# One product for each block of scores in a perceiver's third attention over its context

## The reference

```python
q = x_n @ Wq.T                      # 512 x 256, 16 heads of 16
k, v = split(ctx @ Wkv.T)           # 1601 keys of each batch, 16 heads of 16
p = softmax(q_h @ k_h.T * 16**-0.5) # for each batch and head: 64 x 1601
x = x + concat(p @ v_h) @ Wo.T
```

## Time and profile before

| | |
|---|---|
| median of 3 runs | 2267.64 us (2262.94 to 2269.9) |
| profiled execution, its own time | 2266.19 us |
| its span, first to last instruction | 2264.4 us |
| mean granted TensorE clock | 0.955 |
| PE busy | 2049.1 us (90%) |
| DVE busy | 1389.0 us (61%) |
| ACT busy | 1131.4 us (50%) |
| POOL busy | 507.4 us (22%) |
| score passes, lines 611 to 613 on `cTh`, `cTl`, all three attentions | 768 each, 276.2 + 268.4 + 268.8 us |
| value passes, same lines on `pTh`, `pTl` | 1248 each, 383.5 + 348.4 + 348.0 us |

### The profile page before, as it was taken

The page is one execution under the profiler, slowest core; times in us unless marked ns, Lnnn a source line. Parts: engine busy times, 40 slices in busy tenths (PEclk is TensorE's granted clock), DMA queues, the critical chain, the costliest instruction groups (busy, mean ns, idle before and its releaser), DMA issues. The chain is left out here.

```text
span 2264.4 us, 42645 instructions
## 1 busy us (share of the span) xinstructions
PE 2049.1 (90%) x15334; PEld 1775.2 (78%) x15334; DVE 1389.0 (61%) x2707; ACT 1131.4 (50%) x2279; POOL 507.4 (22%) x410
## 2 busy tenths in 40 slices
PE   5887999999887998489899999987979999999898
PEld 2765999999666875287799999966859999997687
DVE  7465777777455453721677777745447777775466
ACT  3245666666423432321566666624446666664254
POOL 2322222221012420101322222012332122220034
PEclk9798999999997998789999999999989999999999
DMA  5153101100141213531101100002220010000022
GB/s 214 37 237 118 45 31 32 44 30 0 36 149 58 99 34 138 214 146 56 45 31 36 40 30 30 0 17 72 75 93 32 31 43 32 30 15 0 19 79 77
DMA packets 32317, 144.06 MB, mean 64 GB/s; under 512 B 3632, under 2 KB 9136, under 8 KB 28848
## 3 DMA queue, kind: packets, MB, share of 16 engines
q1 hardware_dynamic: 32176, 142.23, 17.5%
HBM read 125.59 MB, written 13.90 MB: 62 GB/s over the span
## 5 line engine op out<-in xcount | busy, mean ns | idle before, releaser
L1021 ACT ACTIVATE pTh<-ps 128x512 fp32r<-128x512 f32 (+1 forms) x768 | 353.9, 519 | 384.2 <-PE ps L921 382.0
L1079 DVE TENSOR_TENSOR pTl<-ps,pTh 128x512 fp32r<-128x512 f32 (+1 forms) x768 | 416.0, 583 | 128.4 <-ACT pTh L1021 128.1
L611 PE MATMUL ps<-pTh,ch 128*128 128x256 f32 (+1 forms) x1248 | 383.5, 307 | 2.6 <-DVE pTl L1079 2.5
L612 PE MATMUL ps<-pTl,ch 128*128 128x256 f32 (+1 forms) x1248 | 348.4, 279 | 0.0
L613 PE MATMUL ps<-pTh,cl 128*128 128x256 f32 (+1 forms) x1248 | 348.0, 279 | 0.0
L611 PE MATMUL ps<-cTh,qh 128*128 128x512 f32 (+2 forms) x768 | 276.2, 360 | 20.7 <-POOL ql L875 13.5
L613 PE MATMUL ps<-cTh,ql 128*128 128x512 f32 (+2 forms) x768 | 268.8, 350 | 0.0
L612 PE MATMUL ps<-cTl,qh 128*128 128x512 f32 (+2 forms) x768 | 268.4, 349 | 0.0
L1066 DVE TENSOR_REDUCE top<-ps 128x1 f32<-128x802 f32 x192 | 189.4, 986 | 111.1 <-PE ps L613 111.1
L611 PEld LDWEIGHTS ps<-pTh,ch 128*128 128x128 f32 (+1 forms) x1248 | 235.1, 188 | 16.7 <-DVE pTl L1079 12.8
L612 PEld LDWEIGHTS ps<-pTl,ch 128*128 128x128 f32 (+1 forms) x1248 | 235.7, 189 | 0.0
(11 more groups left out here) (349 smaller groups left out, 3645.1 us busy)
## 6 DMA issues: line engine op xcount, KB each, us to landing
w<-l1f_w_in SPq DMA_DIRECT2D x16, 1024.0 KB, 8.2
raw<-ctxT_in SPq DMA_DIRECT2D x16, 801.0 KB, 4.2
raw<-ctx_in SPq DMA_DIRECT2D x14, 832.0 KB, 4.5
wg<-l0f_guide_in SPq DMA_DIRECT2D x10, 704.0 KB, 5.1
z<-ctx_in SPq DMA_DIRECT2D x8, 832.0 KB, 12.8
z<-z SPq DMA_DIRECT2D x8, 832.0 KB, 10.8
keys<-ctx_in SPq DMA_DIRECT2D x8, 832.0 KB, 10.2
zT<-zT SPq DMA_DIRECT2D x8, 801.0 KB, 8.8
```

The lines of the kernel that those rows point to most:

```text
L611: pe.matmul(out, high, moving_high, start=start, stop=False)
L612: pe.matmul(out, high, moving_low, start=False, stop=False)
L1021: nc.scalar.activation(pTh[0:w, PARTS[g][0]:PARTS[g][0] + n, slot, :], ps[0:w, turned_bank[slot][g], 0:n * P].rearrange("p (k r) -> p k r" ...
L1079: dve.tensor_tensor(pTl[0:w, at, slot, :], ps[0:w, turned_bank[slot][g], 0:n * P].rearrange("p (k r) -> p k r", r=P), pTh[0:w, at, slot, : ...
```

## The change

Only `l3x` changes. The first and second of the three attentions go on using `cross_attention`.

- **Real keys.** Keys of a batch are projected: `project_keys` multiplies the transposed context by `wk`, three passes for each of 8 tiles (2 chunks of 128 key features, 4 tiles of some 400 keys). ACT copies a tile out of PSUM bank 7 (`keep_key`), POOL splits it (`split_key`), and SP moves it.
- **The stack.** Two heads have 32 key features together. `stacked` holds for each pair of heads 96 rows: the high part, the high part again, the low part. `move_half` fills them with 12 DMAs of 32 rows from SBUF to SBUF, 48 a batch. `stacked` exists once, so a chunk's moves wait until its four units are scored.
- **The queries.** Each pair's query is repeated three times in the rows of the product (`wq` is laid out so), and ACT or DVE copies it out of PSUM twice, masked for either head (the last operation of each: `tensor_scalar` or `activation` with a mask as scale). `stage` makes rows 0 to 31 high, 32 to 63 low and 64 to 95 high. One matmul over 96 rows then gives high·high + low·high + high·low.
- **Order.** In a couple PE runs `key_tile` 0 ahead of `values(1)`, behind a wait for `low(1)` since both use bank 7, and `key_tile` 1 behind the odd scores. ACT's two `keep_key` stand behind second keep 3. The last batch has no tiles.
- **Raw context.** POOL does both parts of its split; ACT's copies go. The transposed context has one buffer instead of two.
- **Setup.** The two dense steps become one block in which PE makes 8 query products and 8 key tiles of batch 0; the first scores wait for all 48 moves. The next layer's weights (`l3a`) are loaded after the attention instead of before, since their room serves as `high` and `raw`.

```diff
...
+        qs = keys.qs[0:STACK].rearrange("p (i n) -> p i n", i=2)
+        probs = normed[:, 0:KEYS], rooms[:, 0:KEYS]
...
+        def key_tiles(i, at, final):
+            return () if final and i else tuple((at // 2, 2 * (at % 2) + j, j) for j in range(2))
...
+                def move(b, at):
+                    sp.wait_ge(key_low, 8 * b + 2 * at + 2)
+                    sp.sem_inc(move_seen, 1)
+                    if at % 2 == 0:
+                        sp.wait_ge(scores_ready, 8 * b + 4 + 2 * at)
+                    move_half(sp, keys, key_highs, key_lows, at // 2, at % 2, moved[at % 2])
+                def batch(b, final=False):
+                    fetch_rows(b + 1)
+                    move(b, 0)
+                    move(b, 1)
+                    if not final:
+                        fetch_keysT(b + 2)
+                    move(b, 2)
+                    move(b, 3)
+                sp.dma_start(raw[:, 0:KEVEN], dram["ctxT"][1]).then_inc(raw_landed, 16)
+                batch(0)
+                with sp.Fori(1, B - 2) as b:
+                    batch(b)
+                batch(B - 2, True)
...
+                def stage(c, batch, k, early):
+                    if not early:
+                        pool.wait_ge(scores_ready, 2 * (c - 1))
+                        pool.sem_inc(high_seen, 1)
+                    heads, at = slice(4 * (k % 4), 4 * (k % 4) + 4), bass.ds(batch * S, S)
+                    pool.tensor_copy(qs[:, k % 2].rearrange("p (h s) -> p h s", s=S), q[0:STACK, heads, at])\
+                        .then_inc(high_staged, 1)
+                    pool.wait_ge(high_staged, c + 1)
+                    pool.sem_inc(high_seen, 1)
+                    pool.tensor_tensor(qs[32:64, k % 2].rearrange("p (h s) -> p h s", s=S), q[32:64, heads, at],
+                                       qs[32:64, k % 2].bitcast(F32).rearrange("p (h s) -> p h s", s=S),
+                                       ALU.subtract).then_inc(staged, 1)
...
+                def split_key(n, tile):
+                    cols = K_COLS[tile]
+                    pool.wait_ge(key_kept, n + 1)
+                    pool.sem_inc(key_seen, 1)
+                    pool.tensor_copy(key_highs[:, cols], key_rows[:, cols]).then_inc(key_high, 1)
+                    pool.wait_ge(key_high, n + 1)
+                    pool.sem_inc(key_seen, 1)
+                    pool.tensor_tensor(key_lows[:, cols], key_rows[:, cols], key_highs[:, cols].bitcast(F32),
+                                       ALU.subtract).then_inc(key_low, 1)
...
+                def body(step, first, final=False):
+                    for k in range(COUPLES):
+                        i, at = k // 4, k % 4
+                        c, b = step * COUPLES + k, 2 * step + i
+                        if not (final and k == COUPLES - 1):
+                            stage(c + 1, 2 * step + (k + 1) // 4, (k + 1) % COUPLES, first and k < 1)
+                        if first and k == 0:
+                            split_raw(1, keys.cTh[:], keys.cTl[:])
+                        for chunk, tile, j in key_tiles(i, at, final):
+                            split_key(8 * b + 2 * at + j, tile)
+                        if at == 1 and not (final and i):
+                            if first and i == 0:
+                                pool.wait_ge(keys.first_moved[1], 2 * MOVES)
+                            else:
+                                pool.wait_ge(value_ready, 4 * b)
+                            split_raw(2 * b + 2, ch[:, 1 - i], cl[:, 1 - i])
+                        if at == 3 and not final:
+                            split_raw(2 * b + 3, keys.cTh[:], keys.cTl[:])
...
+                        chunk = (u % PER) // 4
+                        if first and i == 0:
+                            if u == 0:
+                                for sem in keys.first_moved:
+                                    pe.wait_ge(sem, 2 * MOVES)
+                        else:
+                            for sem in moved:
+                                pe.wait_ge(sem, MOVES * (2 * (2 * step + i) - 1 + chunk))
+                    if u % 2 == 0:
+                        pe.wait_ge(staged, step * COUPLES + u // 2 + 1)
+                    k, at = (u // 2) % 2, (u % 2) * P
+                    for n in range(4):
+                        if n in (0, 2) and not (first and u == 0):
+                            pe.wait_ge(probs_ready if n else probs_half, v)
+                        last = pe.matmul(flat[:, score_cols[n]], qs[:, k, at:at + P],
+                                         keys.stacked[:, u % PER, score_cols[n]], start=True, stop=True)
+                        if n == 1:
+                            last.then_inc(scores_half, 1)
+                    last.then_inc(scores_ready, 1)
...
+                def key_tile(u, step, j, final):
+                    i, at = u // PER, (u // 2) % 4
+                    for chunk, tile, n in key_tiles(i, at, final):
+                        if n == j:
+                            if at == 0 and j == 0:
+                                pe.wait_ge(low_ready, 2 * (2 * step + i) + 1)
+                            if j == 1:
+                                pe.wait_ge(key_kept, 8 * (2 * step + i) + 2 * at + 1)
+                            project_keys(pe, keys, chunk, tile, 7).then_inc(key_ready, 1)
+                def key_bank_free(u, step, final):
+                    i, at = u // PER, (u // 2) % 4
+                    if key_tiles(i, at, final):
+                        pe.wait_ge(key_kept, 8 * (2 * step + i) + 2 * at + 2)
...
+                        pe.wait_ge(probs_half, v)
+                        turn_second(0, v - 1)
+                        scores(u, step, first)
+                        if first and u == 2:
+                            key_bank_free(0, step, final)
+                        turn_second(1, v - 1)
+                        turn_second(2, v - 1)
+                        values(0, c - 1, i, first and u == 2, new_batch)
+                        turn_second(3, v - 1)
+                        if key_tiles(u // PER, (u // 2) % 4, final):
+                            pe.wait_ge(low_kept, 4 * v - 2)
+                        key_tile(u, step, 0, final)
+                        values(1, c - 1, i)
+                        scores(u + 1, step, first)
+                        key_tile(u, step, 1, final)
+                        turn_first(0, v)
+                        turn_first(1, v)
+                        values(2, c - 1, i)
+                        key_bank_free(u, step, final)
+                        turn_first(2, v)
+                        values(3, c - 1, i)
+                        turn_first(3, v)
...
+                def keep_key(step, first_step, i, at, tile, j):
+                    b = 2 * step + i
+                    act.wait_ge(key_ready, 8 * b + 2 * at + j + 1)
+                    if j == 0 and at >= 2:
+                        act.wait_ge(moved[at % 2], MOVES * (2 * b + 1))
+                    if j == 0 and at < 2 and not (first_step and i == 0):
+                        act.wait_ge(moved[at % 2], MOVES * 2 * b)
+                    cols = K_COLS[tile]
+                    nc.scalar.activation(key_rows[:, cols], ps[:, 7, 0:cols.stop - cols.start], ACT.Copy)\
+                        .then_inc(key_kept, 1)
...
+                        if before:
+                            keep(0, v - 1, 1)
+                            keep(1, v - 1, 1)
+                            keep(2, v - 1, 1)
+                        exponents(v, 0, first and u < 2, 0)
+                        exponents(v, 0, first and u < 2, 1)
+                        if before:
+                            keep(3, v - 1, 1)
+                            for chunk, tile, j in tiles:
+                                keep_key(step, first, i, at, tile, j)
+                        keep(0, v, 0, c if before else None)
+                        keep(1, v, 0, c if before else None)
+                        exponents(v + 1, 1, first and u < 2, 0)
+                        exponents(v + 1, 1, first and u < 2, 1)
+                        keep(2, v, 0, c if before else None)
+                        keep(3, v, 0, c if before else None)
...
+K_COLS = [slice(0, 402), slice(402, 802), slice(802, 1202), slice(1202, KEVEN)]
+K_HALVES = slice(0, 802), slice(802, KEVEN)
+STACK = 3 * 32
+MOVES = 16 * 12
+def move_half(sp, keys, high, low, chunk, half, moved):
+    cols = K_HALVES[half]
+    for j in range(4):
+        rows = slice(32 * j, 32 * j + 32)
+        for n, src in enumerate((high, high, low)):
+            sp.dma_start(keys.stacked[32 * n:32 * n + 32, 4 * chunk + j, cols].bitcast(F32), src[rows, cols].bitcast(F32)).then_inc(moved, 16)
+def project_keys(pe, keys, chunk, tile, bank):
+    cols = K_COLS[tile]
+    at = slice(chunk * P, chunk * P + P)
+    return three_passes(pe, ps[:, bank, 0:cols.stop - cols.start], keys.wkh[:, at], keys.wkl[:, at],
```

(69 more changed lines are left out.)

279 lines of the change are left out of this document (271 added, 8 removed).

## The result

| | before | after |
|---|---|---|
| median, runs of both side by side | 2269.9 us (5 runs, 2262.94 to 2276.82) | 2287.77 us (5 runs, 2286.26 to 2292.49) |
| ratio, 95% interval | | 1.008 (1.0059 to 1.0101) |
| profiled execution, its own time | 2266.19 us | 2292.49 us |
| its span | 2264.4 us | 2290.7 us |
| PE busy | 2049.1 us (90%) | 2019.4 us (88%) |

The change makes the kernel 0.8% slower, although TensorE has 30 us less to do. That closeness is partly luck: three terms of the sum were off, the setup by +3.0 us, the first couple by +1.1 and the loop by -3.1, and they cancel to +1.1.

What follows compares the result with a forecast made beforehand. The prediction took a dependence loop, as long as TensorE's full work, to bound the kernel. Setup +25.8, first couple +1.5 and loop -9.5 gave +17.8 us on the profiled 2266.19: 2284, range 2236 to 2304.

Steps and rivals of the forecast that it cites:

- What bounds the kernel: Third attention: a loop of dependences of 12.06 us a couple and TensorE's equally long work are two coinciding limits.
- Rival (a): Third attention's loop: TensorE's work really bounds, so couples fall to 10.46 us and the kernel to 2239; chance 0.17.
- Scores: Score blocks: TensorE loses 2.84 us a couple, the loop only 1.42, since even units' scores are not on it.
- Key projections: Two key tiles a couple, both on the loop, add 1.24 us; couples with keys become 11.88.
- ScalarE, VectorE: Key keeps, about 0.46 us each, fall in ScalarE's idle time; VectorE's loop work is unchanged.
- Last batch: Couples without key tiles: `exponents` waits for `maximum` instead, and a couple takes 11.03 us.
- GpSimd: Key-tile splits take 1.8 us each with waits; a batch costs 30 of 47.5 us, so they are covered.
- The moves: Transfers of 32 rows on SP's queue: 0.55 us each, hidden in the loop until 0.78 us a transfer.
- Setup: Before the loop: first score waits for splits and 48 transfers, coming at 1710.3 us, +25.8.
- First couple: After the setup's wait the clock is at 0.50 for a few us: +1.5 us, bounds 0 to 4.
- Rival (b): Loop, at `keep_key` of tile 0: moves slower than 0.78 us become the wait; 2342 at 1.0 us; chance 0.11.
- Rival (c): Loop: TensorE idle 1.5 us a couple gets its clock granted at half, costing over 200 us; chance 0.02.

Runs made afterwards that it cites:

- e1: The changed kernel with each odd unit's score block multiplied three times instead of once: 2333.44 us, ratio to before 1.0268.
- e2: The changed kernel with each even unit's score block multiplied three times instead of once: 2286.84 us, ratio to before 1.0081.
- b3: The kernel before with all units' scores in the third attention high·high only: 2229.07 us, ratio 0.9815.
- b1: The kernel before with only the odd units' scores in the third attention cut to high·high: 2233.48 us, ratio 0.9843.
- b2: The kernel before with only the even units' scores in the third attention cut to high·high: 2271.0 us, ratio 1.0001.
- e4: The changed kernel with key tile 0 moved behind the even scores, and turns, keeps, moves and splits reordered to suit: 2283.84 us, ratio to before 1.0042.
- e6: The changed kernel with both the edits of e3 and e4: 2270.67 us, ratio to before 0.999.
- e7: e6 with half of chunk 0's setup moves issued on ScalarE's queue, ahead of its copies of chunk 1's tiles: 2273.33 us, ratio to before 0.9997.
- e8: e6 with chunk 0's last 6 setup moves on ScalarE behind its key-tile copies, and two chunk 1 splits on VectorE: 2270.06 us, ratio to before 0.9992.
- e5: The changed kernel with the second chunk's 24 setup moves issued by ScalarE's queue: 2284.53 us, ratio to before 1.005.
- e3: The changed kernel with the second chunk's 24 first moves issued inside the attention, awaited only at the fifth unit: 2278.48 us, ratio to before 1.0019.

## Why the prediction held, point by point

- **What bounds the kernel.** Right. The loop of dependences, not the sum of TensorE's work, sets the couple (e1 against e2, b3 against b1). Rival (a), couples of 10.46, is refuted: even with a third of the score products and no key tiles they are 10.87 (b3).
- **Scores.** Right in both halves: 0.74 for one pass, as the distance in the timeline after, and only the odd unit's counts (b2, e2: zero). At b1 I expected 10.65 and met 10.87, since below that the chain changes its last member from the transposes to `maximum`.
- **Key projections.** Right place, slightly dear: 11.88 was forecast, 11.6 to 11.9 measured. Tile 1 takes 0.56 and tile 0 0.66 (1855.53 to 1856.19). I had charged each a switch of 0.06, and the scores another; the scores and tile 1 show none. In the couple shown that is 0.08 of the 0.09 us between forecast and 11.79. The loop's term was -9.5, measured -12.6: the 26 periods with keys gave -8.4 where -4.7 was forecast, the four behind them -4.6 where -3.8 was, and the last stretch to the last store grew by 0.5 (7.22 to 7.70) where 0.9 was to be saved. Why the last stretch grew was not traced; it grew in b1 and b3 as well (7.61 and 7.65) and not in b2 (7.25) or e1 (7.31), so it goes with the odd units' single pass.
- **ScalarE, VectorE.** Right: the two key copies stand in ScalarE's idle time and the chain from keep(0) on has before's lengths (0.97, 2.45, 1.40, 2.04).
- **Last batch.** 11.03 forecast, 10.9 measured (10.50 once), by the named cause: `exponents` waits for `maximum`, and starts 2.74 us behind the odd scores' start (2.9 forecast).
- **GpSimd.** A split of a key tile takes 1.44 to 1.6 in the setup, I had 1.8: I scaled it from rows of other shapes and added waits. It was covered either way.
- **The moves.** The term that was mis-sized. I priced a move by its transfer, 0.55 from the overlapped pair of the earlier trace rows, and had the issue of the same row, 0.62 to 0.65, as upper bound. Measured 0.636: the issue binds, and the step of the working that took the transfer as the pace was wrong. The transfer is in fact cheaper than I had it, 0.42, which only two queues can show. So the 185 GB/s of `v<-v`, which I set beside the page's 189, is not shown to be the rate of the 32 rows' ports: two queues moved 245. In the loop they stayed hidden, as forecast.
- **Setup.** +25.8 forecast, +28.8 measured: 48 x (0.636 - 0.55) = 4.1, less 1.1 for the faster splits. With 0.636 in it the sum would have been 2288. The 2.1 us that I added for the last move to land had the right size and the wrong cause: they went into entering the attention and staging the first queries.
- **First couple.** +1.5 forecast, +2.6 measured; inside the bounds of 0 to 4. The clock stood at 0.50 through the wait, as foreseen, but it stayed there for 17 us behind the first score (1719 to 1736) and not for a few.
- **Rival (b)** did not occur in the change, but its waits did in e4, e6, e7 and e8, where the moves are due earlier.
- **Rival (c)** is refuted: with TensorE busy for 43.48 of 48 us the granted clock was 1.00; b3, at 41.79 of 48, kept 1.00 too.
- **Left open.** One period some 2 us longer than its neighbours stands in the middle of the stage, in before too (13.87 there, 14.36 after), but not in e5 and e7 (11.82, 11.79), and in e6, e7 and e8 there are one or two more, up to 15.97. In before ScalarE stood idle 1.82 us in it (1877.9 to 1879.7) for nothing that the profile shows. In after its keep started 1.53 us behind the transposes, where it is 0.69 elsewhere, TensorE was busy for 0.38 of 2 us, and the clock fell to 0.50 behind that. In e6 to e8 ScalarE waits 8 to 9 us for moves, 3.5 at most at a time; how much of the extra periods that makes was not traced. Such periods move single profiles by a few us, so stages are to be compared at that grain.

## What to carry to other kernels

An engine at 100% and a chain of dependences of the same length are two limits; halve the engine's work and the chain still stands. Before trading work on the full engine for work elsewhere, follow one period of the loop and mark which of the removed instructions lie on the chain: here half of them, and the replacements lay on it entirely. A pipeline's first filling is paid in full unless part of it can be put off, as in e3, so price many small transfers by the issue on their queue as well as by their bytes, and when moving issues to another queue look at what stands behind them there.

## What the runs showed of the hardware

- A DMA from SBUF to SBUF of 32 rows of 3.2 KB takes 0.59 to 0.64 us of its queue where only one queue issues, on SyncE and on ScalarE alike; in after's attention the loads of whole context tiles from HBM take 0.33 to 0.36, once 0.42 and once 0.59. One queue so moves 148 to 163 GB/s at a DMA share of 0.63 to 0.70. The Trainium skill has this case (Perfetto Trace Analysis, section 'What "DMA-bound" means'): where the issuing engine's track is solid with DMA slices, descriptor generation binds and not the movement. The trace agrees: SyncE's track is solid for 30.5 us of the setup with the DMA engines at 0.67 to 0.70, and a second queue raised the rate (e7).
- Two queues together moved 245 GB/s in e7 and 218 in e5, 1.4 to 1.6 times one queue. The Trainium skill (SBUF — State Buffer, section "Can I just issue two DMAs to hit both halves?") says that two concurrent DMAs are served one after the other and gave only 6% over one. These runs differ from that, for small transfers whose issue binds; large ones were not run. Nor does the 1.8 us that the prediction estimated from the same page for 64 KB transfers hold here: the moves overlap, at 0.636 each on one queue and 0.42 on two.
- TensorE's clock was granted at 1.00 (its 2.4 GHz) from 1800 to 1848 us with a wait in every couple, down to 41.79 busy of 48 us. It was granted at 0.50 (1.2 GHz) within the 25 us wait of after's setup and for 17 us behind the first score, and once in the loop, from 1914 to 1916 us, behind 2 us in which TensorE was busy for 0.38.
